# The second expert layer makes its rows two pairs at a time, over four row strips and four column strips

## The reference

```python
perm = (logits == jnp.max(logits, axis=-3, keepdims=True)).astype(x.dtype)
dispatched = jnp.einsum('bgtd,bgtes->bgesd', grouped, perm)
inner = jax.nn.relu(jnp.einsum('bgesd,desf->bgesf', dispatched, f1) + bias)
intermediate = jnp.einsum('bgesf,esfd->bgesd', inner, f2)
out = jnp.einsum('bgesd,bgtes->bgtd', intermediate, perm)
```

## Time and profile before

| what | value |
|---|---|
| median of 3 runs | 1158.83 us (1158.22 to 1161.05) |
| the profiled execution | 1153.65 us |
| its span, first to last instruction | 1151.5 us |
| mean granted TensorE clock | 0.993 |
| PE / DVE / ACT / POOL busy | 96% / 76% / 51% / 44% |
| L802, matmuls of the second layer | 2048 records, first at 1043.3 us |
| L654, ACT's copies of pairs | 60, 1017 ns each |

### The profile page before, as it was taken

How to read it: one execution, slowest core, us unless ns; L and a number is a source line. 1 busy time by engine, 2 the same in 40 slices (tenths; PEclk the granted TensorE clock), 3 DMA queues, 4 the chain that set the end, 5 groups by cost and what they waited for, 6 DMA issues and landing times.

```text
span 1151.5 us, 27876 instructions
## 1 busy us (share of the span) xinstructions
PE 1102.3 (96%) x10904; PEld 766.5 (67%) x10904; DVE 869.9 (76%) x2215; ACT 592.5 (51%) x1099; POOL 509.6 (44%) x721
## 2 busy tenths in 40 slices
PE   7999999999999999999999999999999997778996
PEld 6788888888566555555555555565688886775454
DVE  6756776675588888778878887786588886777877
ACT  4222222222566666666666666667444433446774
POOL 1000000010677888777778877777466650000334
PEclk9999999999999999999999999999999999999899
DMA  8878897769754446666444566622499985852867
GB/s 285 303 270 279 306 344 245 249 233 277 199 121 116 114 112 143 148 147 127 116 114 114 123 148 148 148 69 75 141 327 308 307 275 156 242 165 58 263 223 224
DMA packets 164096, 223.36 MB, mean 194 GB/s; under 512 B 10240, under 2 KB 90624, under 8 KB 163968
## 3 DMA queue, kind: packets, MB, share of 16 engines
q1 hardware_dynamic: 163968, 221.62, 65.4%
HBM read 143.69 MB, written 77.63 MB: 192 GB/s over the span
## 4 chain that ended last, share of the span: by engine, by line
PE 84%; DMA 8%; DVE 3%; SPq 1%; issue 1%; ACT 1%; POOL 0%; DVEq 0%; POOLq 0%
PE p_bank L1632 14%; PE p_bank L1652 12%; PE p_bank L1671 12%; PE p_bank L1686 7%; PE p_bank L1710 7%; PE p_bank L1712 7%; PE p_bank L1711 7%; PE p_bank L802 4%; DMA kept_f<-in_f 3%; PE p_bank L388 2%; PE p_bank L353 2%; PE p_bank L351 2%; PE p_bank L352 2%; PE p_bank L813 2%; DMA kept_raw<-x_mid_norm 2%
## 5 line engine op out<-in xcount | busy, mean ns | idle before, releaser
L1542 ACT ACTIVATE p_t<-p_bank 128x512 f32<-128x512 f32 (+1 forms) x608 | 303.2, 590 | 123.2 <-PE p_bank L1652 122.1
L1405 DVE CUSTOM_DVE_ANT_0 tried<-p_bank,ban 128x512 bf16<-128x512 f32 (+3 forms) x512 | 229.4, 487 | 92.5 <-PE p_bank L1632 92.3
L1632 PE MATMUL p_bank<-k_stack,q_stack 96*128 96x512 f32 (+3 forms) x768 | 233.8, 364 | 1.2 <-ACT p_t L1542 0.9
L1652 PE MATMUL p_bank<-q_stack,k_stack 97*128 97x512 f32 (+3 forms) x768 | 216.6, 352 | 1.7 <-DMA q_stack<-m_row 1.2
L1632 PEld LDWEIGHTS p_bank<-k_stack,q_stack 96*128 96x128 f32 x768 | 135.6, 189 | 73.2 <-issue 33.5
L1408 DVE TENSOR_REDUCE mx_ab<-p_bank 128x1 f32<-128x512 f32 x256 | 163.8, 683 | 0.0
L1671 PE MATMUL p_bank<-p_t,v_tile 128*32 128x512 f32 (+3 forms) x1536 | 163.0, 492 | 0.6 <-POOL p_t L1285 0.6
L1289 POOL TENSOR_SCALAR_AFFINE_SELECT p_t<-p_t 128x128 f32<-128x128 f32 (+2 forms) x288 | 102.6, 361 | 126.1 <-ACT p_t L1542 118.0
L1652 PEld LDWEIGHTS p_bank<-q_stack,k_stack 97*128 97x128 f32 x768 | 133.1, 189 | 29.8 <-ACT p_t L1542 6.0
L1300 POOL TENSOR_TENSOR p_sum<-p_sum,p_t 128x512 f32<-128x512 f32 x120 | 150.7, 1292 | 0.0
L597 POOL TENSOR_TENSOR kept_o_sum<-kept_o_sum,kept_x_in 128x512 f32<-128x512 f32 x21 | 27.1, 1292 | 171.6 <-ACT kept_o_sum L660 168.0
(11 more groups left out here) (133 smaller groups left out, 2065.7 us busy)
## 6 DMA issues: line engine op xcount, KB each, us to landing
q_stack<-q_hi SPq DMA_DIRECT2D x64, 256.0 KB, 6.4
k_stack<-k_hi SPq DMA_DIRECT2D x30, 512.0 KB, 9.6
kept_f<-in_f SPq DMA_DIRECT2D x24, 512.0 KB, 4.9
x_in<-in_x SPq DMA_DIRECT2D x8, 1024.0 KB, 10.3
x_t<-in_x_t SPq DMA_DIRECT2D x8, 1024.0 KB, 8.9
k_hi<-k_hi_s SPq DMA_DIRECT2D x8, 1024.0 KB, 6.1
k_lo<-k_lo_s SPq DMA_DIRECT2D x8, 1024.0 KB, 8.0
v_rows<-v_out SPq DMA_DIRECT2D x8, 1024.0 KB, 7.7
```

Of the source, the lines that this page charges most:

```text
L1405: dve.tensor_tensor_reduce(scrap, got, ban0[:] if i == 0 else ban[:, CH - w:CH], 1.0, -3e38, ALU.add, ALU.max, to[:, col:col + 1]).then_in ...
L1542: act.activation(pt[:, k % SLOTS_P, u * m:(u + 1) * m, 0:w], bank[:, RINGS["score", n][0], 0:m * w].rearrange("p (m w) -> p m w", m=m), AC ...
L1632: pe.matmul(bank[:, to, 0:w], qs[it % SLOTS][0:R, i * P // CH, h, i * P % CH:i * P % CH + P], ks[it % SLOTS][0:R, h, t0:t0 + w], start=Tru ...
L1652: mm = pe.matmul(bank[:, to, h % m * w:(h % m + 1) * w], ks[slot][0:R + 1, h, j * P:(j + 1) * P], qs[slot][0:R + 1, sh, h, CH - w:CH], sta ...
```

## The change

`make` takes `mp`, two pairs at once. It waits for the buffers of both, then issues 32 fp32 matmuls in the order i, c, q: neighbours go to different row strips, over all four, and to four banks, since the pair of `q // 2` chooses the buffer and `q % 2` the bank in it. The last matmul raises `made` by 2, and the outer loops step over `mp`. The matmuls themselves, their number and what they read and write are the same.

```diff
-        def make(u, pair):
+        def make(u, mp):
 
-            b, h, mp, qp = u % B, u // B, pair // 2, pair % 2
-            n = u * PAIRS + pair
+            b, h = u % B, u // B
+            n = u * PAIRS + 2 * mp
...
             if u == 0:
                 pe.wait_ge(active, mp * 2 + 2)
-            if n >= RING:
-                y_kept(pe, n - RING)
-            else:
-                pe.wait_ge(inner_done, (KD - 1) * NQ + n * 2 + 2)
+            for made_before in (n, n + 1):
+                if made_before >= RING:
+                    y_kept(pe, made_before - RING)
+                else:
+                    pe.wait_ge(inner_done, (KD - 1) * NQ + made_before * 2 + 2)
             for i in range(2):
-                for q in range(qp * 2, qp * 2 + 2):
-                    part = slice(q * F, (q + 1) * F)
-                    for c in range(4):
-                        e = (mp * 2 + i) * 4 + c
-                        mm = pe.matmul(bank[c * GT:(c + 1) * GT, n % RING * 2 + q % 2, i * DH:(i + 1) * DH],
+                for c in range(4):
+                    e = (mp * 2 + i) * 4 + c
+                    for q in range(4):
+                        part = slice(q * F, (q + 1) * F)
+                        mm = pe.matmul(bank[c * GT:(c + 1) * GT, (n + q // 2) % RING * 2 + q % 2, i * DH:(i + 1) * DH],
                                        inner[part, e, b * GT:(b + 1) * GT], f2[e // PIECE][part, e % PIECE],
                                        start=True, stop=True, tile_position=(q * F, c * GT), skip_group_check=True)
-            mm.then_inc(made, 1)
+            mm.then_inc(made, 2)
...
-        for pair in range(PAIRS):
-            make(0, pair)
+        for mp in range(PAIRS // 2):
+            make(0, mp)
         for u in range(UNITS):
-            for pair in range(PAIRS):
+            for mp in range(PAIRS // 2):
                 if u + 1 < UNITS:
-                    make(u + 1, pair)
-                if u > 0 and pair % 2 == 1:
-                    combine((u - 1) * WS + pair // 2)
+                    make(u + 1, mp)
+                if u > 0:
+                    combine((u - 1) * WS + mp)
```

## The result

| | before | after |
|---|---|---|
| median of the runs | 1158.66 us (1157.1 to 1161.16) | 1169.64 us (1165.19 to 1170.08) |
| after / before | | 1.0086, 95% interval 1.0061 to 1.011 |
| profiled execution, its span | 1153.65, 1151.5 | 1169.28, 1167.1 |
| first record of the second layer to the end of the span | 108.1 us | 121.5 us |

The change costs 11 us by the medians (10 by the ratio, with 7 to 13 as its interval), where 2.3 were forecast. (Lines have moved by one: L803 is the second layer's matmul, L814 the combining product.) Of the 15.6 us between the two profiled executions, 2.2 lie ahead of the second layer, where nothing was changed and where the runs differ by as much anyway.

The account below looks back on a forecast made before the run. TensorE paces the last 108 us today; afterwards a TensorE-ACT loop of 2.66 us would. Opening +3.6, +3.05 after the transfers, +0.4 hand-over, -1.15 for the last units: +2.3 on 1158.83, so 1161.1 us, range 1154.5 to 1166.

Parts of the forecast that it names:

- the clock: Second layer's opening: priced without a term for a lower clock, though 1.1 us of idle was expected in every 2.66.
- the steady part: Last three units: +0.4 us for later hand-over to ACT, then -1.15 from units of 10.64 to 10.68 instead of 11.06.
- The couple: 32 fp32 matmuls of two pairs: with 17 in flight, the last starts 1.12 us after the first, 1.42 before.
- Rival (a): Array takes all passes as they come: last start at 0.76 us, total 1154.9 us; chance 0.18.
- (b): 16 tiles with four row strips no faster than 8: last start 1.42 us, loop 2.96, total 1168.3 us; chance 0.10.
- The ring's loop: Next couple waits for ACT's copy of the one before: period 1.60 + 1.01 + 0.05 = 2.66 us.
- The opening by that loop: First units, couples every 2.66 us: first combining product at 1066.3 instead of 1062.78, +3.6 us, the largest term.
- Rival (c): Idle in the opening lowers the granted clock: some four couples cost 1.3 us more each, +5, total 1166.4; chance 0.05.
- Section B: First combining product to the couple waiting for f2's last transfer: period 2.66 for 2.77, -0.3 to -0.5 us.
- The sum: Whole kernel: DVE ends its last unit 2.3 us later, tail as before, so 1161.1 us; forecast's chance 0.60.

Follow-up runs that it names:

- e1: Changed kernel with the old order of matmuls, pair after pair over eight tiles, keeping the grouping and waits: 1180.32 us against 1158.68.
- e4: Wide order, but pairs waited for and given out one by one, a pair's second half mixed with the next pair's first half: 1155.57 us, ratio 0.9961.
- e8: Ring of three, first halves of both pairs ahead of second halves, second buffer's wait behind the first eight matmuls: 1152.17 us against 1157.78 for the kernel before.
- e2: Changed kernel with two spare fp32 matmuls behind each couple of the first two units, to fill TensorE's idle time: 1164.25 us, ratio 1.0044.
- e3: Changed kernel with a fourth buffer while the first two units are made: 1159.82 us, ratio 1.0006.
- e7: Fourth buffer in the opening, first halves of both pairs ahead of second halves, second wait behind eight matmuls: 1153.77 us against 1158.08 for the kernel before.
- e6: Changed kernel leaving out half of the rows (i = 1) in units 5 to 7, so its output is wrong: 1161.77 us in one run.
- e10: e8 with the wait for the second pair's buffer moved ahead of the couple: 1168.49 us against 1157.74 for the kernel before.
- after_again: The changed kernel run once more, unaltered: 1168.96 us, ratio 1.0094 to the kernel before.
- e5: Kernel before with only the order inside each pair turned, c outside and q inside: 1159.13 us against 1158.08.
- e9: Kernel before with a fourth buffer in units 0 and 1 only: 1157.75 us against 1157.78.

## Why the forecast was wrong, step by step

The step that failed is the fourth, the clock; the fifth, the steady part, lacked a term as well.

**The couple: right.** 17 fp32 matmuls in flight, last record at 1.12: measured 1.11. Rival (a), an array that takes all passes at 0.76, and (b), 16 tiles no better than 8, are both out; e1 has (b)'s last start, 1.41, only with the old order on eight tiles, and e4's 1.38 fits the same limit. (The prediction counts the 17 as 68 instructions and calls that an agreement with the figure it cites; the two are four apart, and no run here says why.)

**The ring's loop: right in sum.** 2.66 forecast, 2.68 measured, with two small errors that cancel. ACT begins 1.52 and not 1.60 after the couple; the way from ACT's start to the next couple takes 1.16, not 1.06. The 0.05 for the semaphore came from a load with work queued around it, and e8's loop has it again; where TensorE stands at the wait with nothing queued, its first load starts 0.12 after the copy's end (1050.87 - 1050.75) and its first matmul record 0.15 (1.16 - 1.01).

**The opening by that loop: right as far as it goes.** The first product comes 22.9 us behind the first record, as e2 has it. (The prediction's couples at 1048.9 and 1051.6 stand up to 0.2 behind steps of 2.66, and 1066.3 - 1062.78 is 3.5, not 3.6; this changes nothing.) That the supply of instructions leaves little to win there held too: e3 and e7, with the wide array and a buffer more, have an A of 18.9 and 18.3 where the kernel before has 19.4, and idle times put down to issue are left in it.

**The clock: the step that failed.** The sum took the whole opening at full clock, with 1.1 us of idle in every 2.66: a term of nothing, where e2 measures 5.4 us. Rival (c) named the mechanism, the place and 5 us, and I gave it 0.05. In the opening the fall came in all five profiles of kernels that wait ahead of the couple, with the ring of three and nothing to fill the gap (after and its repeat, e1, e6, e10), and in none of the others. It cost five couples 3.56 - 2.68 = 0.88 each, 4.4 us, and a combining product at 1.94 for 1.11 at its end; e2 says 5.4 us in all. Rival (c)'s 1.3 for a couple came from eight tiles (e1: 4.29 - 2.98 = 1.31), so its +5 is right in part by luck: fewer couples for more each. The prediction gives no reason for so low a chance. The row beside it, 0.66 behind 1.9 us of idle, is of a wait that came once, and this one stands in every couple. The Trainium skill has this case in "TensorE: Matmul & The Clock Gate" (A second HAM failure mode: psum-queue depth-cycling): an engine that idles briefly and often between groups of matmuls, as it cycles through its banks, has its clock throttled and restored in turn. The traces agree on the fall, with 1.2 us idle in 2.68, but not on the turns: here the clock fell once, stayed at 0.50 (from 1055.6 to 1076.1, in after_again from 1048.3 to 1075.6) and came back only behind the first combining product. I ought to have weighed it.

**The steady part: a term left out.** From the transfers' end I had summed -1.15 for faster periods and +0.4 for a later hand-over; C and D together are 57.0 us for 53.8 before, +3.2. Between stops the period is 2.68 as forecast, but over C it is 35.3 / 12 = 2.94. The stops are put down to issue. They show inside the couples: over C the couples' last records start 3.0 us in all behind the 1.11 of an undisturbed couple, and C is too long by 35.33 - 12 x 2.68 = 3.2. Half the instructions (e6) remove them, and a wait that stands behind the first eight matmuls leaves one (e8 against e10). An instruction packet lies in front of the stop at 1119.61 (DMA queues in 1117 to 1119.7: packets, MB, share), and none in 1119.7 to 1121.8:
```profile
q8 instruction: 1, 0.02, 2.2%
```
The page doesn't say for which engine it is, but the times do. In the changed kernel such packets landed at 1089.54, 1118.34 and 1122.83, and the loads of the stopped couples resumed at 1091.13, 1119.61 and 1124.22, which is 1.3 to 1.6 us later. So it is in every kernel that stops. From 8 us behind the first combining product on, all traces together have 37 waits of the couples' loads for issue that are longer than 0.45 us, and 35 of them end 1.2 to 1.6 us after a packet of queue 8 has landed, although such packets are 3.3 us or more apart. (The two others are in e1.) The stops are therefore very likely TensorE's program running out of instructions; no experiment changed the supply alone. Why a program that stands at a wait with nothing queued is served worse stays open.

**Section B.** Here I had -0.5 and the changed kernel has +2.4: 0.8 to 1.3 for the clock's recovery, 1.00 for the stop at 1090.12. Part of the rest is the profile of before itself: e5 and e9, whose periods and times are those of before, have 37.0 and 38.7 where it has 34.9. There the clock was at 0.50 just behind the first combining product, from 1065.6 to 1069.0 and from 1063.9 to 1070.8. Busy time by stretch, e9 and then before:
```profile
1063.00:1073.00 10.00, 10.00 (x194) 4.81 (x202) 8.02 (x8) 6.86 (x8) 2.55 (x2) 0.66 0.29 84
```
```profile
1063.00:1073.00 10.00, 10.00 (x299) 5.74 (x298) 9.74 (x10) 8.80 (x11) 2.59 (x2) 1.00 0.41 135
```
The idle time ahead of that product was 2.17 us in e9 and 1.61 in e5, where the clock fell, and 1.89 before, where it did not. I had taken the stretch of one favourable execution as the kernel's.

**The sum.** Forecast +2.3, measured +11.0. The clock is 5.4 of the difference (e2). With it held the kernel stands at 1164.25, 3.1 above the forecast's 1161.1. These 3.1 are a remainder and no measurement of their own, so that 2.3 + 5.4 + 3.1 = 10.8 is no check. What is seen in e2's profile is of this size: C is 33.7 - 12 x 2.68 = 1.5 us too long, and the last couple's last record comes 1.8 late, by this stop:
```profile
1141.42 1.28 PE L803 MATMUL p_bank<-kept_f,kept_inner 32*32 32x256 f32 x38 [1.32 <-issue]
```

## What to carry to other kernels

A wait that is moved ahead of a group of work costs more than its own loop: find out what the engine still has queued while it waits, and put the wait as late as the data allow, in the middle of the group if need be (16 us here, for one line). Where a change opens a short idle time in every turn of a loop on TensorE, price the whole stretch at half clock and give that case a real chance. When several things are given out at once, look whether the ring still lets the producer run ahead: here one buffer more in the opening was worth 9.8 us to the changed kernel (e3) and nothing to the kernel before (e9).

## What the hardware showed that was not expected

- TensorE's clock fell to 0.50 with idle times of only about 1 us between couples, after as few as two couples (after_again: 1.19 us idle in 2.68; e10: 1.06 in 2.54), and stayed there for the rest of the opening. In the openings of e2, e3, e4, e7 and e8 it stayed at 1.00, in e4 and e8 with idle times of up to 0.47 us in couples about 1.97 apart. Longer idle times, of up to 2.50 us, lie ahead of the second layer in the changed kernel and in e3 alike, so they don't make the difference.
- At half clock a couple takes 2.37 for 1.48 us on 16 tiles and 3.09 for 1.78 on 8. The loop's waits for ACT (1.19 us) don't change, so a period grows from 2.68 to 3.56 and from 2.98 to 4.29, and does not double.
- The order of packed fp32 matmuls matters within the limit of 17: the same 32 of a couple have their last record at 1.11 or 1.12 (wide order, or first halves ahead of second halves), 1.38 (halves mixed) or 1.41 to 1.42 (eight tiles at a time).
- A couple could stop in its middle for about 1 us though its buffers were free and its data there, as behind its 15th record at 1118.47 in the changed kernel. It went on 1.2 to 1.6 us after an instruction packet had landed.
